# A gather that waits in mid-quad: two graph-attention layers with indirect DMA on Trainium2

## The chip, the core and the metric

The kernel runs on one NeuronCore of a Trainium2 chip. A core has five engines with a queue of instructions each: TensorE (PE in the profile, its weight loads PEld), VectorE (DVE), ScalarE (ACT), GpSimd (POOL) and SyncE (SP). They run side by side and wait for each other by semaphores only. Sixteen DMA engines move data between the chip's main memory (HBM) and the core's scratch memory (SBUF). The metric is the device time of one execution in microseconds (us), the median of several runs.

## The reference

A graph has 6250 nodes with 128 features and 106250 edges, sorted by target node. The first layer is an attention over the edges with 8 heads, followed by a feed-forward block; the second is another attention with 4 heads. Both have the same shape. Cut to what matters here, for the first:

```
q_dst = Q[dst] + rel_q[edge_type]
k_src = K[src] + rel_k[edge_type] + (time_emb @ Wt + bt)
v_src = V[src] + rel_v[edge_type]
euclid = sum(q_dst * k_src) / sqrt(DH) * decay
hyp    = -hyp_beta * norm(m[src] - m[dst]) * decay
logits = alpha * euclid + (1 - alpha) * hyp
attn   = softmax of logits over the edges with the same dst
agg    = segment_sum(v_src * attn, dst)
```

and for the second:

```
combined = leaky_relu(x_src[src] + x_dst[dst] + edge_emb[edge_type])
logits   = einsum(combined, att)
attn     = softmax of logits over the edges with the same dst
agg      = segment_sum(x_src[src] * attn, dst)
```

The rows that belong to `src` are scattered in memory, so they are gathered: one index, one row.

## The kernel before, in words

Edges are cut into tiles of 128, and four tiles (QS = 4) make a quad. A pass over all edges has 221 quads. There are two passes: `edges0` for the first layer and `edges1` for the second. Between them lie the joining of tiles and the work on nodes (`join_tiles`, `nodes0`), ahead of them the making of the tables (`front`), behind them `join_tiles` again and `nodes1`.

In a pass GpSimd does nothing but gather. For each quad it issues four indirect DMAs (line L1106 in the first pass, L1838 in the second), one for each tile. One gather fetches 128 rows from `d_table0` (384 floats each, 196.6 KB in all) or `d_table1` (132 floats each, 67.6 KB in all). All four add 16 to one semaphore, `rows_in[c % ring]`; it has its full value when all four have landed in SBUF. The rows go to a ring of 12 quads in the first pass (RQ0) and of 16 in the second (RQ). The names `gathered0` and `gathered` are these semaphores.

GpSimd waits for two things ahead of the first gather of a quad: that ScalarE has copied the indices (`idx_in`, once in four or eight quads) and that the quad which held the ring's slot is done (`sums`, which TensorE raises when it has summed that quad: two steps for a quad). Then comes a step on the semaphore `passed` that nobody waits for (`apart`), and the four gathers.

The other engines work on quad c in this order. TensorE's `edge(c)` waits for `rows_in` of the quad and adds gathered rows and rows of the target node, picked by a one-hot matmul, in PSUM (L1321 to L1333, L2014 and L2016). VectorE multiplies, reduces to logits and builds one-hots (L1161 to L1172, L1879 to L1898). Some quads later (LAG0 = 7 in the first pass, LAG = 10 in the second), with the weights of the softmax known, VectorE scales the values (L1196, L1895) and TensorE sums them by target (L1345, L2040). This raises `sums`. ScalarE copies the sums out of PSUM (L1275, L1981), and VectorE adds them to the accumulator (L1150, L1908). SyncE brings one-hot sources for two quads (first pass, L1058) or for eight quads (second pass, L1809 and L1811) as a broadcast of one row to 120 partitions.

Each pass is written as a head of two ring lengths, a hardware loop whose body is one ring length, and a tail, and so each engine has its own loop branch. The order of the instructions on each engine is the order in which the code emits them; no scheduler moves them.

Of the kernel before, what the change touches and what calls it, by code (L numbers as in the profile page):

```python
# [31 lines left out]
QS = 4  # L32
# [8 lines left out]
RQ = 16  # L41
# [3 lines left out]
LQ0, RQ0, LAG0, NQN = 4, 12, 7, 2  # L45
# [35 lines left out]
def apart(eng, passed):  # L81


    eng.sem_inc(passed, 1)
# [870 lines left out]
def nth0(i, c, per=1, plus=0):  # L955

    v = c * per + plus
    return v if i is None else i * (RQ0 * per) + v


def edges0(nc, k):
# [11 lines left out]
    with ExitStack() as ctx:  # L973
# [32 lines left out]
        rows_in = k.gathered0  # L1006
# [10 lines left out]
        def group(i, c, per=1, plus=0):  # L1017
            v = c // LQ0 * per + plus
            return v if i is None else i * (RQ0 // LQ0 * per) + v
# [5 lines left out]
        def quads(i, c0, emit):  # L1025
            for c in range(c0, c0 + (RQ0 if c0 else HEAD)):
                emit(i, c)
# [8 lines left out]
        with nc.Block() as block:  # L1036
# [60 lines left out]
            @block.gpsimd  # L1097
            def _(pl):
                def gather(i, c):
                    if c % LQ0 == 0:  # L1100
                        pl.wait_ge(idx_in, group(i, c, 1, 1))
                    if i is not None or c >= RQ0:
                        pl.wait_ge(sums, nth0(i, c - RQ0 + 1, 2))
                    apart(pl, k.passed)
                    for t in range(QS):
                        nc.gpsimd.indirect_dma_start(  # L1106
                            rows[:, c % RQ0 * QS + t, 0:3 * D], None, k.d_table0,
                            bass.IndirectOffsetOnAxis(ap=idx[c // LQ0 % 3][:, c % LQ0 * QS + t:c % LQ0 * QS + t + 1], axis=0))\
                            .then_inc(rows_in[c % RQ0], 16)

                quads(None, 0, gather)
                with pl.Fori(0, NITER) as i:
                    quads(i, HEAD, gather)
                for c in range(TAIL, sz.quads):
                    gather(None, c)
# [617 lines left out]
def nth(i, c, per=1, plus=0):  # L1733

    v = c * per + plus
    return v if i is None else i * (RQ * per) + v


def edges1(nc, k):
# [8 lines left out]
    with ExitStack() as ctx:  # L1748
# [27 lines left out]
        rows_in = k.gathered  # L1776
# [7 lines left out]
        def quads(i, c0, emit):  # L1784
            for c in range(c0, c0 + (RQ if c0 else HEAD)):
                emit(i, c)
# [11 lines left out]
        with nc.Block() as block:  # L1798
# [29 lines left out]
            @block.gpsimd  # L1828
            def _(pl):
                def gather(i, c):  # L1830
                    if c % LQ == 0:
                        pl.wait_ge(idx_in, c // LQ + 1 if i is None else i * 2 + (c // LQ + 1))
                    if i is not None or c >= RQ:
                        pl.wait_ge(sums, nth(i, c - RQ + 1, 2))
                    apart(pl, k.passed)
                    for t in range(QS):
                        r = c % RQ * QS + t
                        nc.gpsimd.indirect_dma_start(  # L1838
                            rows[:, r, :], None, k.d_table1,
                            bass.IndirectOffsetOnAxis(ap=idx[c // LQ % 2][:, c % LQ * QS + t:c % LQ * QS + t + 1], axis=0))\  # L1840
                            .then_inc(rows_in[c % RQ], 16)

                quads(None, 0, gather)
                with pl.Fori(0, NITER) as i:
                    quads(i, HEAD, gather)
                for c in range(NQUAD - RQ, sz.quads):
                    gather(None, c)
# [631 lines left out]
```

## Time and profile before

| | us |
|---|---|
| median of 3 timed runs | 3782.01 |
| lowest and highest of them | 3778.65, 3783.29 |
| span of the profiled execution | 3808.8 |
| first pass, first to last gather | 317.5 to 1830.5 |
| second pass, first to last gather | 2236.0 to 3602.8 |
| GpSimd busy in the whole span | 1924.7 (51%) |
| TensorE busy in the whole span | 2583.3 (68%) |
| VectorE busy in the whole span | 2475.7 (65%) |

The span runs from the first to the last instruction of one execution under the profiler; for that execution there is no other time. It is 26.8 us (0.7%) longer than the median of the timed runs. No engine is busy for three quarters of the span, so what matters is what the engines wait for. A line of a timeline has the start, the duration, the engine, the line of the code, the operation with what it writes and reads, and in brackets the idle time of that engine before it with what ended it. "remote" and "issue" there mean that the trace shows no releaser of its own; a releaser is inferred and can be another than the one named. The ends of matmuls are modelled.

### The profile page before, as it was taken

Reading aid. Unit: us, or ns where it says so; the run is one execution under the profiler, and the core shown is the slowest. Engines: PE = TensorE matmul, PEld = TensorE weight load, DVE = VectorE, ACT = ScalarE, POOL = GpSimd, SP = SyncE. Lnnn points to the kernel's source line nnn. Section 1 sums busy time; section 2 is a strip of 40 time slices with the busy share of each in tenths; the row PEclk is TensorE's granted clock in tenths of the full one; section 3 lists DMA queues with packets and bytes.
Section 4 is the critical chain, followed back from the end, with each engine's and each line's share of the span. In section 5 each row is a group of like instructions: output and inputs, shape, how many; then the busy total and the mean of one; then the engine's idle time right before and its main releaser. Section 6 shows DMA issues by size and latency. Waiting matters only on the chain. (4 is left out here: it accounts for less than half of the span.)

```text
span 3808.8 us, 60179 instructions
## 1 busy us (share of the span) xinstructions
PE 2583.3 (68%) x13302; PEld 1992.9 (52%) x13303; DVE 2475.7 (65%) x5935; ACT 1131.3 (30%) x3887; POOL 1924.7 (51%) x1957
## 2 busy tenths in 40 slices
PE   4893777777777777787668844666666566666654
PEld 3572555555555555565444423555555555555553
DVE  6443677677776767677755543666666666666678
ACT  2441444434343434444325520111111111111115
POOL 1004455555555555556330045666666666666554
PEclk9896888888888888898689977778788788878765
DMA  5475455555555555555301132333332333333221
GB/s 103 95 221 170 123 156 149 154 146 156 146 154 148 152 150 145 151 155 156 93 3 27 27 71 61 68 68 69 64 70 62 66 69 69 69 69 69 52 52 34
DMA packets 253667, 386.96 MB, mean 102 GB/s; under 512 B 70853, under 2 KB 168881, under 8 KB 249642
## 3 DMA queue, kind: packets, MB, share of 16 engines
q0 software_dynamic: 86432, 239.62, 24.7%
q1 hardware_dynamic: 132662, 130.96, 13.8%
q10 hardware_dynamic: 34260, 13.43, 1.4%
q14 instruction: 266, 2.18, 0.2%
q8 instruction: 47, 0.77, 0.1%
HBM read 342.88 MB, written 40.92 MB: 101 GB/s over the span
## 5 line engine op out<-in xcount | busy, mean ns | idle before, releaser
L1838 POOL DMA_INDIRECT pair<-d_table,e_idx x884 | 886.8, 1003 | 780.6 <-ACT e_idx L1962 300.6
L1106 POOL DMA_INDIRECT pair<-d_table,e_idx x884 | 870.5, 985 | 649.8 <-issue 238.6
L2040 PE MATMUL e_p_r<-pair,e_oh 128*122 128x132 f32 x1768 | 332.1, 342 | 425.5 <-DVE pair L1895 319.3
L1321 PE MATMUL e_p_t<-e_wbd,e_feat 128*128 128x512 f32 x442 | 289.1, 741 | 385.4 <-DVEq L1170 296.7
L2040 PEld LDWEIGHTS e_p_r<-pair,e_oh 128*122 128x122 f32 x1768 | 280.3, 233 | 467.3 <-issue 356.9
L1981 ACT COPY pair<-e_p_r 122x264 f32<-122x264 f32 x442 | 160.0, 380 | 994.2 <-DMA pair<-in_xT 471.9
L2014 PE MATMUL e_p_x<-pair,iden 128*128 128x264 f32 x884 | 342.8, 477 | 104.0 <-issue 63.2
L2016 PEld LDWEIGHTS e_p_x<-big,e_oht 128*128 128x128 f32 x1768 | 331.6, 232 | 48.9
L1325 PEld LDWEIGHTS e_p_q<-big,e_oht 128*128 128x128 f32 x1768 | 281.1, 226 | 136.5 <-issue 136.5
L1879 DVE SCALAR_TENSOR_TENSOR e_prod<-e_p_x,e_att 128x512 f32<-128x512 f32 x221 | 151.0, 683 | 271.6 <-remote 232.6
L2016 PE MATMUL e_p_x<-big,e_oht 128*128 x1768 | 325.6, 315 | 0.0
L1275 ACT COPY e_bound<-e_p_r 122x272 f32<-122x272 f32 x442 | 154.9, 387 | 512.6 <-remote 343.7
L1333 PEld LDWEIGHTS e_p_m<-big,e_oht 128*128 128x128 f32 x1768 | 240.2, 196 | 127.3 <-issue 127.3
L1283 ACT ACTIVATE e_p_m<-e_p_m 128x128 f32<-128x128 f32 x884 | 234.2, 265 | 205.1 <-ACT e_bound L1275 95.2
L1321 PEld LDWEIGHTS e_p_t<-e_wbd,e_feat 128*128 128x128 f32 x442 | 77.5, 219 | 406.3 <-issue 322.7
L1150 DVE TENSOR_TENSOR big<-big,e_bound 120x136 f32 x884 | 259.4, 293 | 36.5 <-issue 17.2
L1325 PE MATMUL e_p_q<-big,e_oht 128*128 x1768 | 279.1, 310 | 0.0
L1166 DVE TENSOR_TENSOR pair<-pair,e_p_q 128x512 f32<-128x512 f32 x221 | 150.5, 681 | 191.3 <-remote 187.5
L1908 DVE TENSOR_TENSOR big<-big,pair 120x132 f32 x884 | 217.6, 294 | 85.4 <-ACT pair L1981 39.9
L1161 DVE TENSOR_TENSOR pair<-pair,e_p_t 128x512 f32<-128x512 f32 x221 | 151.9, 687 | 183.9 <-issue 122.6
L1345 PE MATMUL e_p_r<-pair,e_oh 128*122 128x136 f32 x1768 | 251.7, 286 | 19.4 <-DVE pair L1196 10.1
L1331 PE MATMUL e_p_m<-pair,iden 128*128 128x512 f32 x442 | 256.9, 667 | 0.0
(362 smaller groups left out, 4518.6 us busy)
## 6 DMA issues: line engine op xcount, KB each, us to landing
pair<-d_table,e_idx POOLq DMA_INDIRECT x1768
e_node<-d_node SPq DMA_DIRECT2D x28, 960.0 KB
e_node<-d_node SPq DMA_DIRECT2D x111, 240.0 KB
d_table<-tab_kmv SPq DMA_DIRECT2D x54, 360.0 KB
e_feat<-in_edge_attr ACTq DMA_DIRECT2D x442, 16.0 KB
e_feat<-in_edge_attr SPq DMA_DIRECT2D x442, 16.0 KB
e_gate<-d_gate SPq DMA_DIRECT2D x84, 64.5 KB
d_decay<-pair SPq DMA_DIRECT2D x7, 512.0 KB, 4.1
```

The lines of the kernel that those rows point to most:

```text
L1106: nc.gpsimd.indirect_dma_start(rows[:, c % RQ0 * QS + t, 0:3 * D], None, k.d_table0, bass.IndirectOffsetOnAxis(ap=idx[c // LQ0 % 3][:, c % ...
L1150: last = V.tensor_tensor(to, to, bound[a // BQ % 3][0:BN, a % BQ * QS + t, :].unsqueeze(1), ALU.add)
L1283: last = A.activation(p_m[c % 2][:, t, :], p_m[c % 2][:, t, :], ACT.Square, accum_out=d2[c // LQ0 % 3][:, c % LQ0 * QS + t:c % LQ0 * QS + ...
L1321: M(p_t[:, :, :].rearrange("p t d -> p (t d)"), feat[c % 6][:, :], wbd[:, :, :].rearrange("p t d -> p (t d)"), start=True, stop=True).then ...
L1325: last = M(p_q[:, t, :], oht[c % 3][:, t * P:(t + 1) * P], qm[:, bass.ds(of[t], 1), 0:D], start=True, stop=True)
L1331: M(m[:, :, :], k.iden[:, :], rows[:, r:r + QS, D:2 * D], start=True, stop=False)
L1333: last = M(m[:, t, :], oht[c % 3][:, t * P:(t + 1) * P], qm[:, bass.ds(of[t], 1), D:2 * D], start=False, stop=(t == QS - 1))
L1345: last = M(p_r[h][0:R_LAST + 1, t - 2 * h, 0:W], oh[w % 2][:, t, :], rows[:, w % RQ0 * QS + t, 2 * D:R0], start=True, stop=True)
L1838: nc.gpsimd.indirect_dma_start(rows[:, r, :], None, k.d_table1, bass.IndirectOffsetOnAxis(ap=idx[c // LQ % 2][:, c % LQ * QS + t:c % LQ * ...
L2014: M(x[:, 2 * h:2 * h + 2, 0:W], k.iden[:, :], rows[:, r + 2 * h:r + 2 * h + 2, :], start=True, stop=False)
L2016: last = M(x[:, t, 0:W], oht[c % 4][:, t * P:(t + 1) * P], xd[:, bass.ds(held["blocks"][(c - 1) % 4 * QS + t if c else t], 1), :], start=F ...
L2040: last = M(p_r[h][0:R_LAST + 1, t - 2 * h, 0:W], oh[w % 2][:, t, :], rows[:, w % RQ * QS + t, :], start=True, stop=True)
```

## The change

In both passes GpSimd gets one more wait ahead of the third of the four gathers of quad c: until `rows_in` of quad c-1 has its full value, so until the four gathers of the quad before have landed. A step on `passed` follows it. The very first quad of a pass has no such wait. `slot` works out the value for the first pass; in the second it is written out.

```
@@ first pass
                     apart(pl, k.passed)
                     for t in range(QS):
+                        if t == QS // 2 and (i is not None or c >= 1):
+                            pl.wait_ge(rows_in[(c - 1) % RQ0], slot(i, c - 1, RQ0, 16 * QS))
+                            apart(pl, k.passed)
                         nc.gpsimd.indirect_dma_start(
                             rows[:, c % RQ0 * QS + t, 0:3 * D], None, k.d_table0,
@@ second pass
                     for t in range(QS):
                         r = c % RQ * QS + t
+                        if t == QS // 2 and (i is not None or c >= 1):
+                            b = c - 1
+                            pl.wait_ge(rows_in[b % RQ], 16 * QS * (b // RQ + 1) if i is None else i * (16 * QS) + 16 * QS * (b // RQ + 1))
+                            apart(pl, k.passed)
                         nc.gpsimd.indirect_dma_start(
                             rows[:, r, :], None, k.d_table1,
```

On GpSimd's queue this reads as follows in the loop of the first pass, from the loop's top. `e0_idx_in` is `idx_in`, `e0_sums` is `sums`, and `gathered0` with a number is `rows_in` of that slot. Before:

```order
L1112 ISA
L1103 ISA [waits e0_idx_in]
L1106 DMA pair<-d_table,e_idx 128x384 [waits e0_sums]
L1106 DMA pair<-d_table,e_idx 128x384 x3
L1103 REGISTER_ALU
L1106 DMA pair<-d_table,e_idx 128x384 [waits e0_sums]
L1106 DMA pair<-d_table,e_idx 128x384 x3
```

Now:

```order
L1115 ISA
L1103 ISA [waits e0_idx_in]
L1109 DMA pair<-d_table,e_idx 128x384 [waits e0_sums]
L1109 DMA pair<-d_table,e_idx 128x384
L1107 ISA
L1109 DMA pair<-d_table,e_idx 128x384 [waits gathered011]
L1109 DMA pair<-d_table,e_idx 128x384
L1103 REGISTER_ALU
L1109 DMA pair<-d_table,e_idx 128x384 [waits e0_sums]
L1109 DMA pair<-d_table,e_idx 128x384
L1107 REGISTER_ALU
L1109 DMA pair<-d_table,e_idx 128x384 [waits gathered00]
```

A quad's four gathers in a row are now two and two, with a wait and one register instruction between them. Nothing changes places, and no other engine's queue changes.

In the second pass the same stands in the loop. There the semaphores have numbers that earlier stages used under other names: `tab_x_in0` is `sums` and `tab_decay_out3` is `idx_in` of this pass. Before:

```order
L1838 DMA pair<-d_table,e_idx 128x132 [waits tab_x_in0]
L1838 DMA pair<-d_table,e_idx 128x132 x3
L1838 DMA pair<-d_table,e_idx 128x132 [waits tab_decay_out3,tab_x_in0]
L1838 DMA pair<-d_table,e_idx 128x132 x3
L1838 DMA pair<-d_table,e_idx 128x132 [waits tab_x_in0]
```

Now:

```order
L1851 ISA
L1837 ISA [waits tab_decay_out3]
L1845 DMA pair<-d_table,e_idx 128x132 [waits tab_x_in0]
L1845 DMA pair<-d_table,e_idx 128x132
L1843 ISA
L1845 DMA pair<-d_table,e_idx 128x132 [waits gathered15]
L1845 DMA pair<-d_table,e_idx 128x132
L1837 REGISTER_ALU
L1845 DMA pair<-d_table,e_idx 128x132 [waits tab_x_in0]
```

Here too each quad's gathers fall in two pairs, the second of them behind the landing of the quad before.

## Rows read from the trace of the kernel before

**Rows 1.** The page's head and its busy times (section 1).

```profile
span 3808.8 us, 60179 instructions
PE 2583.3 (68%) x13302; PEld 1992.9 (52%) x13303; DVE 2475.7 (65%) x5935; ACT 1131.3 (30%) x3887; POOL 1924.7 (51%) x1957
```

**Rows 2.** Windows over the two passes: length, busy time by engine, clock, DMA share, GB/s.

```profile
core 0: us, PE busy (x) PEld busy (x) DVE busy (x) ACT busy (x) POOL busy (x), PEclk, DMA share, GB/s
317.50:1830.50 1513.00, 1130.40 (x6160) 849.41 (x6161) 1059.73 (x2517) 600.09 (x2528) 870.47 (x884) 0.86 0.54 150
2236.00:3603.00 1367.00, 819.25 (x4317) 720.59 (x4317) 864.43 (x2180) 170.07 (x515) 886.76 (x884) 0.79 0.32 68
```

**Rows 3.** GpSimd's waits: line, released by, us in total, times, longest.

```profile
POOL pair L1838 <- issue: 244.1, 776, 2.0
POOL pair L1106 <- issue: 238.6, 727, 3.1
```

**Rows 4.** Waits of VectorE and ScalarE for TensorE's results, whole span.

```profile
DVE e_prod L1879 <- remote: 232.6, 38, 30.7
DVE pair L1166 <- remote: 187.5, 47, 7.0
ACT pair L1981 <- DMA pair<-in_xT: 471.9, 77, 11.8
ACT e_bound L1275 <- remote: 343.7, 103, 7.3
```

**Rows 5.** Timeline of the second pass, around one stall.

```profile
2850.67 0.33 SPq L1809 DMA_DIRECT2D e_node<-d_node  x1
...
2852.85 1.31 POOL L1838 DMA_INDIRECT pair<-d_table,e_idx  x1 [0.30 <-issue]
...
2855.72 0.94 POOL L1838 DMA_INDIRECT pair<-d_table,e_idx  x1 [0.30 <-issue]
...
2856.97 0.94 POOL L1838 DMA_INDIRECT pair<-d_table,e_idx  x1 [0.30 <-issue]
...
2859.43 0.61 PE L2016 MATMUL e_p_x<-big,e_oht 128*128 x4
...
2863.21 0.95 POOL L1838 DMA_INDIRECT pair<-d_table,e_idx  x1 [0.30 <-issue]
2866.20 0.69 DVE L1879 SCALAR_TENSOR_TENSOR e_prod<-e_p_x,e_att 128x512 f32<-128x512 f32 x1 [7.22 <-remote]
2866.38 0.66 ACT L1981 COPY pair<-e_p_r 122x264 f32<-122x264 f32 x2 [11.18 <-DMA pair<-in_xT]
...
2867.07 1.21 POOL L1838 DMA_INDIRECT pair<-d_table,e_idx  x1 [2.91 <-DMA pair<-in_xT]
```

**Rows 6.** Windows over the same place, columns as in rows 2.

```profile
2853.00:2854.00 1.00, 1.00 (x9) 1.00 (x10) 0.81 (x4) 0.28 (x1) 1.00 (x1) 1.00 1.01 217
2856.00:2857.00 1.00, 0.00 (x0) 0.00 (x0) 1.00 (x4) 0.00 (x0) 0.69 (x2) 1.00 1.12 214
2858.00:2859.00 1.00, 1.00 (x10) 0.94 (x9) 0.79 (x2) 0.00 (x0) 0.79 (x1) 1.00 0.68 152
2859.00:2860.00 1.00, 1.00 (x8) 0.79 (x6) 0.00 (x0) 0.00 (x0) 0.69 (x2) 1.00 0.19 50
```

**Rows 7.** Timeline of the first pass: a result taken up while GpSimd stands still.

```profile
1016.24 0.95 POOL L1106 DMA_INDIRECT pair<-d_table,e_idx  x1 [0.30 <-issue]
...
1017.00 1.09 PE L1345 MATMUL e_p_r<-pair,e_oh 128*122 128x136 f32 x8
...
1018.88 1.12 POOL L1106 DMA_INDIRECT pair<-d_table,e_idx  x1 [1.70 <-PE e_p_r L1345]
```

**Rows 8.** Timeline of the first pass: a result made while GpSimd gathers.

```profile
1030.74 1.09 PE L1345 MATMUL e_p_r<-pair,e_oh 128*122 128x136 f32 x8
...
1035.10 0.95 POOL L1106 DMA_INDIRECT pair<-d_table,e_idx  x1 [0.30 <-issue]
1037.66 0.69 DVE L1166 TENSOR_TENSOR pair<-pair,e_p_q 128x512 f32<-128x512 f32 x1 [5.50 <-remote]
1037.89 0.67 ACT L1275 COPY e_bound<-e_p_r 122x272 f32<-122x272 f32 x2 [5.30 <-remote]
```

**Rows 9.** Timeline of the second pass's start: gathers and the matmuls that wait for them.

```profile
2251.63 0.94 POOL L1838 DMA_INDIRECT pair<-d_table,e_idx  x1 [0.30 <-issue]
...
2254.36 0.88 PE L2014 MATMUL e_p_x<-pair,iden 128*128 128x264 f32 x2
```

**Rows 10.** The source line of the broadcast for eight quads.

```profile
L1809 SPq DMA_DIRECT2D e_node<-d_node x28: 330/337/539, 2232.6 to 3533.3; - x28
```

More of the change, by code:

```diff
@@ L1105, in gather @@
                     for t in range(QS):
+                        if t == QS // 2 and (i is not None or c >= 1):
+                            pl.wait_ge(rows_in[(c - 1) % RQ0], slot(i, c - 1, RQ0, 16 * QS))
+                            apart(pl, k.passed)
                         nc.gpsimd.indirect_dma_start(
@@ L1837, in gather @@
                         r = c % RQ * QS + t
+                        if t == QS // 2 and (i is not None or c >= 1):
+                            b = c - 1
+                            pl.wait_ge(rows_in[b % RQ], 16 * QS * (b // RQ + 1) if i is None else i * (16 * QS) + 16 * QS * (b // RQ + 1))
+                            apart(pl, k.passed)
                         nc.gpsimd.indirect_dma_start(
```

## The prediction

> **What bounds the kernel now.** I read the page's head first. No engine is busy for more than 68% of the span [rows 1], so waits decide. Next I asked for windows over the two passes, since only they change: 1513 us and 1367 us, together 2880 of 3808.8 us. With 221 quads each that is 6.85 and 6.19 us per quad. GpSimd is busy for 870 and 887 us of it, so it could finish a quad in 5.0 us (four gathers of 0.95 and four pauses of 0.30), and the DMA engines are busy to 0.54 and 0.32 [rows 2]. In neither pass is GpSimd or the DMA the limit on average.
>
> The view of waits by engine says who is late: VectorE waits 232.6 us at L1879 and 187.5 us at L1166, ScalarE 471.9 us at L1981 and 343.7 us at L1275 [rows 4]. All four lines read PSUM, that is, they wait for TensorE. But TensorE is not at work then either. The timeline shows it best. In the second pass the last matmul of a quad starts at 2859.43; VectorE, which waits for it, starts at 2866.20 and ScalarE at 2866.38. Between them only GpSimd works; its last gather of that series ends at 2864.16, and it too goes on only at 2867.07 [rows 5]. In the first pass the sums are made at 1030.74 to 1031.83, GpSimd gathers until 1036.05, and VectorE and ScalarE go on at 1037.66 and 1037.89 [rows 8]. The opposite case: GpSimd's gather ends at 1017.19, the sums end at 1018.09, and GpSimd itself takes them up 0.79 us later [rows 7]. So a result of TensorE that comes late in an unbroken series of gathers is taken up some 1.6 to 2.0 us after the series has ended, and one that comes while GpSimd rests is taken up at once. Why this is so no row says. I call such a stretch a stall; it is the costliest thing in both passes, and its length goes with GpSimd's series. That is where a wait on GpSimd can act.
>
> **The change part by part.** It adds 220 waits and 220 steps on `passed` to each pass, removes nothing and moves no instruction. Other engines' queues are as before.
>
> The instructions themselves: the pause between two gathers is 0.30 us, and it is also 0.30 us ahead of a quad that needs no wait, where a wait and a step stand already [rows 5]. I cost 440 of them at nothing; GpSimd's own 0.95 us of work on the gather before hides them. Without that cover it would be at most the 0.79 us from a release to the gather's start [rows 7].
>
> Behind the new wait stand the third and fourth gather and the next quad. Who needs them? Quad c is released in the first pass when quad c-12 is summed, in TensorE's step c-4, and read in step c-1, three steps or some 20 us later; in the second pass it is c-6 to c-1, some 31 us. Its gathers take 5 us. A delay of 1 to 4 us is hidden from `rows_in`'s readers.
>
> How long does the wait last? The third gather starts 2.80 us after the end of the last gather of the quad before (0.30 + 1.25 + 1.25) if GpSimd did not rest, and later if it did. The last gather of quad 1 of the second pass ends at 2252.57 and TensorE reads it at 2254.36 [rows 9], so it lands within 1.79 us. With 0.79 us for the release that is 2.58 us: under 2.80, no delay. Of 884 gathers in this pass 776 start after a mere pause, so 108 are behind a wait and 113 quads start without one [rows 3]; all quads are covered while the DMA engines are free. In the first pass the rows are three times as long. No row shows a landing there. From below it is 1.79 us as well; from above I add 129 KB at the 217 GB/s of a full window [rows 6], 0.6 us, and have 2.39 + 0.79 = 3.18 us, a delay of 0.4 us. With the middle, 0.2 us, for the 884 - 727 = 157 waits and so 64 quads without a rest [rows 3], GpSimd loses 13 us of its 640 us of idle time. Where such a quad stands in a stall, the stall lasts that much longer. I take 3 us on the path (from 0 to 26).
>
> The Trainium skill, in DMA: Bandwidth & Descriptors, "Anatomy of one DMA", gives a gather a fixed 2.0 us and its bytes at 436 GB/s, so 2.45 us in the first pass and 2.16 us in the second. By this rule every back-to-back quad would be held, by 0.44 and 0.15 us, in sum some 45 us on GpSimd. The trace has at most 1.79 us in the second pass and disagrees there; for the first pass no row decides.
>
> The exception is the broadcast for eight quads in the second pass. It is issued at 2850.67 [rows 5]; the DMA engines are full at 2853 and 2856 and still at 0.68 at 2858, and only at 2859 down to 0.19 [rows 6]. The last gather of the quad before ends at 2854.16 in the midst of it. I take it to land near 2858, where the load falls off. Then the third gather of the next quad starts at 2858.9 instead of 2856.97: 1.9 us late, behind 2.2 us of rest on GpSimd (0 to 4 us by the same window). A rest of 1.6 to 2.0 us is what lets TensorE's results through. So the series of gathers that ran to 2864.16 is cut in two. Here the result of 2859.4 to 2860 comes two gathers after the rest instead of five or more into a series, and VectorE need not stand for 7.22 us. The second half still has six gathers and ends about 2 us later, so part of a stall can come back. I take 4 us saved of the 7.22 for each such place (bounds: 7.2 saved, 1.9 lost).
>
> How many places? There are 28 broadcasts [rows 10]; one is ahead of the loop. GpSimd is at work in 0.65 of the pass [rows 2], so some 17 of 27 meet a series, and I count 15. That is 15 x 4 = 60 us saved. I expect a third back: time saved makes the series follow each other more closely, and 5.0 us of gathers per quad against 6.19 us leaves little rest. So -60 + 20 + 3 = -37 us.
>
> The profiled span is 26.8 us longer than the median of the timed runs; the sum is a difference, and I apply it to either: 3808.8 to about 3772 in a profile, 3782 to 3745 us timed.
>
> **The rivals.** *Nothing happens.* The waits are met before they are reached, and the rests behind the broadcasts fall where GpSimd would have rested anyway or are too short. For it: 2.58 against 2.80 us, and 20 us of slack. Against it: the full DMA windows. Time: 3782 us.
>
> *Longer stalls, slower.* If a rest of some 2 us inside a series does not let results through (say, because what counts is that GpSimd has nothing left to do), the series just ends later, and every stall with it. The place is the gather series behind a broadcast and the back-to-back quads of the first pass. The price is 27 x 1.9 = 51 us and up to 64 x 0.4 = 26 us. It decides as soon as a delayed series still holds VectorE to its end plus 2 us. With half of both on the path it is +38: 3820 us. For it: both stalls in the rows ended after the series, and I have no row with a rest of 2 us in the middle of one. Against it: [rows 7], where a rest of under 1 us was enough.
>
> *Much faster.* If it is the number of gathers handed over ahead that matters, not GpSimd's rest, then the wait caps it at four in every quad, and stalls shrink everywhere. VectorE's waits of 232.6 and 187.5 us [rows 4] halved give -210: about 3570 us. For it: in the stalls shown GpSimd had the gathers of a further quad in hand, and no row excludes it. Against it: GpSimd's own starts would hardly move, and all that I can see goes by them.
>
> **How the numbers follow.** I give the forecast 0.46, nothing 0.21, slower 0.23, much faster 0.10. About 0.2%, 7.6 us, is what a measurement of this kernel can tell from no change. Faster by more than that is the forecast and the last case, less a little where the gain given back is all of it: 0.54. Within it: 0.23. Slower: 0.23. The forecast's own range is 3700 (all 27 places, 3 us each) to 3774. The range takes in "nothing" and most of "slower": 3690 to 3812 us, with some 0.1 left out on either side.
>
> **What would show it right or wrong.** In the changed kernel's profile the third gather behind a broadcast should have an idle time of about 2 us ahead of it, and there should be 15 to 25 such in the second pass and few over 1 us in the first. VectorE's wait at L1879 (some lines lower now) should fall from 232.6 by about 40 us and ScalarE's at L1981 likewise, and the second pass from 1367 to about 1327 us; the first should stay within 5 us of 1513. If instead the waits at L1879 and L1981 grow with the rests there, the slower rival holds. If the first pass falls by more than 20 us, my account of what ends a stall is wrong, since almost no rest is added there. If no idle time appears ahead of third gathers, the change does not reach the gathers at all.

## The result and the profile after

The changed kernel takes 3818.49 us (median of 4 runs, 3812.17 to 3826.65); the kernel before took 3782.65 us beside it (4 runs, 3778.65 to 3785.65). The ratio is 1.0098, 95% interval 1.0074 to 1.0122: slower by 36 us. A repetition with more runs gave 1.0092 (1.0072 to 1.0112). The forecast was 3745 us, and 3818 lies just above its range.

The page's head, to be held against [rows 1]:

```profile
span 3810.3 us, 60671 instructions
PE 2566.5 (67%) x13302; PEld 1979.6 (52%) x13303; DVE 2470.3 (65%) x5935; ACT 1130.8 (30%) x3887; POOL 1919.9 (50%) x1957
```

The two profiled spans, 3808.8 and 3810.3 us, hide the difference. Before's profiled execution was 27 us longer than its timed median, after's 8 us shorter. So I compare stages, and look how much each scatters among kernels that have it unchanged. The windows over the passes of the changed kernel, columns as in [rows 2]:

```profile
core 0: us, PE busy (x) PEld busy (x) DVE busy (x) ACT busy (x) POOL busy (x), PEclk, DMA share, GB/s
304.70:1796.60 1491.90, 1123.29 (x6158) 841.08 (x6159) 1056.29 (x2519) 600.02 (x2534) 870.27 (x884) 0.89 0.54 152
2198.90:3607.60 1408.70, 822.33 (x4332) 723.27 (x4333) 865.85 (x2185) 171.86 (x517) 881.81 (x884) 0.78 0.30 66
```

The first pass shrank from 1513 to 1492 us. That says nothing: in the 14 other kernels run below with an unchanged first pass it took 1483 to 1533 us. The second pass grew from 1367 to 1409 us; in a run below with the second pass unchanged it took 1356 us, and in two more with the wait 1401 and 1404 us. That is the loss.

GpSimd's waits, to be held against [rows 3] (line, released by, us in total, times, longest):

```profile
POOL pair L1109 <- issue: 264.4, 731, 2.2
POOL pair L1845 <- issue: 240.9, 760, 3.8
...
POOL pair L1845 <- DMA pair<-in_xT: 135.7, 51, 4.4
POOL pair L1845 <- DMA pair<-d_table,e_idx: 90.2, 42, 5.9
...
POOL pair L1109 <- DMA pair<-d_table,e_idx: 20.3, 14, 3.0
```

A releaser is new: the landing of gathers (`pair<-d_table`), 90.2 us in the second pass. By the trace 24 third gathers of that pass have over 1.5 us of idle time ahead of them (median 3.8, longest 5.9 us), 23 of them at quads with c % 8 = 2, behind the broadcast. In the first pass 10 have over 1.5 us.

What waited for TensorE in [rows 4], now:

```profile
DVE e_prod L1886 <- remote: 149.1, 23, 32.3
DVE pair L1169 <- remote: 129.6, 33, 7.1
ACT pair L1988 <- DMA pair<-in_xT: 440.4, 76, 15.4
ACT e_bound L1278 <- remote: 328.0, 106, 6.0
```

All four fell, and yet the kernel is slower. Only one of these falls is clear of the scatter. L1166 (now L1169) and L1275 (now L1278) belong to the first pass, and in the 14 kernels run below with an unchanged first pass the same rows read 123 to 178 us and 244 to 346 us. A row holds one releaser only: over all releasers L1981 waits 992 us before, 978 us in the run below with an unchanged second pass and 981 us now. L1879 over all releasers waits 271 us before and 278 and 280 us in two kernels below without a wait in the second pass, and 220 us now (202 us in the repetition): this fall is real. The time went to other lines. VectorE's waits from 2330 to 3560 us, first of the kernel before:

```profile
DVE e_prod L1879 <- remote: 165.4, 32, 13.5
...
DVE e_fwd L1919 <- DMA pair<-in_xT: 44.7, 8, 11.0
DVE big L1908 <- ACT pair L1981: 37.1, 30, 3.8
DVE big L1908 <- issue: 32.0, 50, 1.8
```

and of the changed kernel:

```profile
DVE e_prod L1886 <- remote: 91.3, 19, 11.4
DVE e_fwd L1926 <- DMA pair<-in_xT: 86.7, 12, 10.7
DVE big L1915 <- ACT pair L1988: 61.3, 30, 6.7
DVE big L1915 <- issue: 55.9, 63, 4.4
```

The wait ahead of the product (L1886) gave 74 us; those of the scan (L1926) and of the additions (L1915) took 42, 24 and 24 us. The scan waits for TensorE's transpose, the additions for ScalarE's copy of TensorE's sums; the releasers named are inferred. So results of TensorE are still late, only others than before. Over the whole second pass VectorE's idle time is 494 us in the kernel before and 480 us in the run below with an unchanged second pass, and 529 to 536 us in the three traces with the wait in every quad.

Where in the period of eight quads this happens: VectorE's step (from one start of L1879, now L1886, to the next; mean over quads 24 to 215, us), by c % 8:

| c % 8 | 0 | 1 | 2 | 3 | 4 | 5 | 6 | 7 | sum |
|---|---|---|---|---|---|---|---|---|---|
| before | 8.37 | 5.40 | 4.72 | 5.28 | 6.76 | 5.18 | 6.87 | 6.60 | 49.2 |
| changed | 9.76 | 7.98 | 5.75 | 6.40 | 6.40 | 4.70 | 4.20 | 5.66 | 50.9 |
| changed, repeated | 10.01 | 8.53 | 4.67 | 6.33 | 6.01 | 5.04 | 4.27 | 5.67 | 50.5 |

On average VectorE reads a quad 19 to 26 us after its last gather has ended, so it works some four quads behind GpSimd, and GpSimd's rest at c % 8 = 2 falls in VectorE's steps 6 and 7. These became 3.6 us shorter, which fits results that come through in the rest. Steps 0 to 3 became 6.1 us longer. One such place in the timeline of the changed kernel:

```profile
3027.36 0.33 SPq L1812 DMA_DIRECT2D e_node<-d_node  x1
...
3029.54 1.31 POOL L1845 DMA_INDIRECT pair<-d_table,e_idx  x1 [0.30 <-issue]
...
3037.49 1.33 POOL L1845 DMA_INDIRECT pair<-d_table,e_idx  x1 [4.12 <-DMA pair<-d_table,e_idx]
...
3050.89 0.27 PE L2040 MATMUL e_p_e<-iden,e_ext 128*128 128x128 f32 x1
...
3059.22 0.94 POOL L1845 DMA_INDIRECT pair<-d_table,e_idx  x1 [0.30 <-issue]
3060.22 0.30 DVE L1915 TENSOR_TENSOR big<-big,pair 120x132 f32 x1 [2.50 <-issue]
...
3063.13 0.27 ACT L1979 COPY pair<-e_p_e 128x128 f32<-128x128 f32 x1 [12.66 <-DMA pair<-in_xT]
...
3064.00 1.18 POOL L1845 DMA_INDIRECT pair<-d_table,e_idx  x1 [3.83 <-DMA pair<-in_xT]
```

The broadcast is issued at 3027.36, the last gather of quad 129 is issued at 3029.54, and GpSimd rests 4.12 us. Then it gathers without a rest from 3037.49 to 3060.16, 18 gathers. ScalarE has stood still for 12.66 us when it goes on at 3063.13; by the trace the result of TensorE that it waits for (L2040) was ready at 3051.16, 12.0 us earlier. GpSimd rests 3.83 us, and the next round begins. The windows of one us over this broadcast:

```profile
3030.00:3031.00 1.00, 1.00 (x10) 0.97 (x9) 0.70 (x4) 0.38 (x1) 0.85 (x1) 1.00 1.03 213
3034.00:3035.00 1.00, 1.00 (x9) 0.98 (x9) 0.70 (x3) 0.28 (x2) 0.00 (x0) 1.00 0.99 89
3035.00:3036.00 1.00, 1.00 (x8) 0.92 (x7) 0.85 (x2) 0.38 (x2) 0.00 (x0) 1.00 0.38 93
3036.00:3037.00 1.00, 0.74 (x6) 0.52 (x4) 1.00 (x3) 0.00 (x0) 0.00 (x0) 1.00 0.00 0
```

The DMA engines (share, the last number but one) are full in the window from 3034, at 0.38 in the one from 3035 and idle in the one from 3036. With 0.79 us from release to start, GpSimd's wait was met at 3036.7. So the gathers land about when the last of the broadcast does.

A series is a run of gathers with no idle time of over 0.5 us between them. In the trace of the kernel before no series that begins in quads 24 to 220 is longer than 12 gathers; in the changed one 10 have 16 or more (nine of 18, one of 22), and all ten begin with the third gather behind a broadcast. I count these, as long series, in each run below.

### The profile page after: what moved, and what is told of

Read it like the earlier page. It is cut to its first block and busy times, and to the rows that moved or that the text cites. A ratio compares the mean times of both kernels' runs of the same rounds, so it can differ in the third digit from the quotient of the medians.

```text
span 3810.3 us, 60671 instructions
## 1 busy us (share of the span) xinstructions
PE 2566.5 (67%) x13302; PEld 1979.6 (52%) x13303; DVE 2470.3 (65%) x5935; ACT 1130.8 (30%) x3887; POOL 1919.9 (50%) x1957
## 5 line engine op out<-in xcount | busy, mean ns | idle before, releaser
L1915 DVE TENSOR_TENSOR big<-big,pair 120x132 f32 x884 | 217.9, 294 | 132.9 <-ACT pair L1988 65.3
L1886 DVE SCALAR_TENSOR_TENSOR e_prod<-e_p_x,e_att 128x512 f32<-128x512 f32 x221 | 151.0, 683 | 220.5 <-remote 149.1
L1278 ACT COPY e_bound<-e_p_r 122x272 f32<-122x272 f32 x442 | 154.9, 387 | 464.9 <-remote 328.0
L1334 PE MATMUL e_p_m<-pair,iden 128*128 128x512 f32 x442 | 249.0, 648 | 0.0
L1336 PE MATMUL e_p_m<-big,e_oht 128*128 x1768 | 237.9, 276 | 8.9 <-issue 8.8
```

The costliest lines, as they stand in the source:

```text
L1334: M(m[:, :, :], k.iden[:, :], rows[:, r:r + QS, D:2 * D], start=True, stop=False)
L1336: last = M(m[:, t, :], oht[c % 3][:, t * P:(t + 1) * P], qm[:, bass.ds(of[t], 1), D:2 * D], start=False, stop=(t == QS - 1))
```

## The experiments

Each change is made to the kernel before unless said otherwise, in the second pass unless said otherwise. Ratios are to the kernel before on the same chip. That kernel took 3776 to 3788 us beside most of them and 3825 us beside one group (the first runs with small transfers, and the rests at c % 8 = 6 and in every second quad), so only ratios are compared. `rest(...)` is short for a wait on `rows_in[c % RQ]` and a step on `passed`.

**Which waits cost.** The wait in the first pass alone:

```diff
@@ edges0 only
+ if t == QS // 2 and (i is not None or c >= 1): wait for rows_in of c-1
```

> The wait in the first pass alone. Theory A (the loss is made in the second pass, where 24 third gathers rest 1.5 to 5.9 us behind the broadcast for eight quads): 3780 us, within 8 us of before. Rival B (the loss is spread over every added wait and step, 440 of them, 36 us): 3800 us. Rival C (the loss is made in the first pass, and the profiled 1513 us of before was an outlier): 3818 us.

Measured: 0.9996 (0.9977 to 1.0015). The wait in the first pass costs nothing.

The wait in the second pass alone:

```diff
@@ edges1 only
+ if t == QS // 2 and (i is not None or c >= 1): wait for rows_in of c-1
```

> The wait in the second pass alone. Theory A (the loss is made there): 3818 us, the whole of the changed kernel's loss. Rival B (every added instruction costs alike): 3800 us. Rival C (the first pass): 3782 us.

Measured: 1.0104 (1.0075 to 1.0132), 11 series of 16 or more. All of the loss is here.

```diff
- if t == QS // 2 and (i is not None or c >= 1):
+ if t == QS // 2 and (i is not None or c >= 1) and c % LQ == 2:
```

> Second pass alone, and of its 220 waits only the 28 of quads c with c % 8 = 2, those behind the broadcast for eight quads. Theory A: 3818 us with 28 waits instead of 440, and rests of 1.5 to 6 us ahead of those third gathers. Rival B: under 3 us more than before. The mechanism of my forecast (a rest inside a series shortens the stall) would show as a time under 3782 us.

Measured: 1.0106 (1.0080 to 1.0132), 8 long series. GpSimd's waits of this run have the landings 22 times:

```profile
POOL pair L1842 <- DMA pair<-d_table,e_idx: 60.7, 22, 5.7
```

```diff
- if t == QS // 2 and (i is not None or c >= 1):
+ if t == QS // 2 and (i is not None or c >= 1) and c % LQ != 2:
```

> Second pass alone, 192 waits: all but those behind the broadcast. Theory A: 3782 us, within 8 us, and no rests ahead of third gathers over 1 us except at one or two quads. Rival A2 (the rest only moves on to the next quad's third gather, c % 8 = 3): rests and a loss of 10 to 30 us. Rival B: 3798 us.

Measured: 1.0020 (0.9997 to 1.0043), 1 long series; 7 third gathers rest over 1 us. So 28 of the 440 waits make the loss, and neither the number of instructions (rival B) nor the waits elsewhere do.

**Is it the large transfer?** The changed kernel with the broadcast in four parts:

```diff
- sp.dma_start(node[u][0:BN, :], <row of 8 quads>.broadcast_to(...)).then_inc(node_in[u], 16)
+ def piece(p):   # a quarter of the columns; for p > 0 ahead of it:
+     sp.wait_ge(oht_built, nth(i, c - LQ + 2 * p))
+     sp.dma_start(node[u][0:BN, a:b], <row>[a:b].broadcast_to(...)).then_inc(node_in[u], 16)
- dve.wait_ge(node_in[u], 32 * ...)
+ dve.wait_ge(node_in[u], 80 * ...)
```

> The changed kernel (the wait in both passes), but SyncE brings the one-hot source for eight quads of the second pass in four transfers of 0.24 MB, two quads of VectorE's work apart, instead of one of 0.96 MB. Theory A (the waits cost time only because the one large transfer holds back the landing of the gathers issued with it): the 23 rests of 1.5 to 6 us become rests of at most 1.5 us and the loss goes: equal to the kernel before with the same four transfers, within 8 us. Rival D (any rest behind a transfer costs, and four transfers make four rests): 3820 us or more.

Measured: 1.0003 (0.9988 to 1.0019), no long series; one third gather rests over 1.5 us. The same kernel on another chip:

> The changed kernel with four small transfers once more, on the chip of the other runs of this call. If the transfer of 0.96 MB is what makes the waits dear: within 0.3% of before. If the earlier result was a matter of its chip: 1.008 or more.

Measured: 0.9997 (0.9979 to 1.0015). With the same waits and a smaller transfer the loss is gone. GpSimd waits for landings as often as in the changed kernel, but briefly:

```profile
POOL pair L1854 <- DMA pair<-d_table,e_idx: 18.4, 49, 2.1
```

The kernel before with the same four parts, as the base:

> The kernel before with the same four transfers, as the base for the run beside it. No added wait. If nobody waits for the landings in time: 3776 us, within 8 us. If the late landings behind the large transfer already cost the kernel before something on TensorE: 5 to 20 us less.

Measured: 1.0005 (0.9987 to 1.0022). The late landings cost nothing where nobody waits for them. And the changed kernel beside other runs:

> The changed kernel once more, since the runs of the four transfers came from a chip on which the kernel before takes 3825 us and not 3776: beside the others of this call. Theory A: 1.010 times before. If the loss were a matter of the chip: within 0.2% on some.

Measured: 1.0092 (1.0072 to 1.0112), 8 long series.

**Does a rest cost by its place, its length, or with the broadcast?** A rest away from the broadcast:

```diff
+ if t == QS // 2 and c % LQ == 6: rest(2 of this quad's gathers landed)
```

> The kernel before with a rest of GpSimd in the second pass away from the broadcast: ahead of the third gather of quads c with c % 8 = 6 it waits until the first two gathers of the same quad have landed (1.3 us median landing and 0.79 us for the release, so about 2 us of rest at 28 places, 50 us of GpSimd's time). Theory A (a rest delays the series, and what stands behind the series is late by as much): 15 to 50 us slower, 3791 to 3826 us. The mechanism of my forecast (a rest of 2 us lets TensorE's results through): faster, 3720 to 3760 us. Theory A1 (a rest costs only when it is much longer than 2 us, since then several quads of slots come free and the next series is 18 gathers long): 3776 us, within 8 us.

Measured: 1.0026 (1.0006 to 1.0046), 1 long series; rests of 2.4 us (median) at 27 places. These 10 us lie between theory A (15 to 50) and theory A1 (at most 8); the time did not fall. The same rest where the changed kernel has it, with small transfers:

```diff
@@ with the broadcast in four parts
+ if t == QS // 2 and c % LQ == 2: rest(2 of this quad's gathers landed)
```

> Small transfers, and a rest of 2.3 us at c % 8 = 2 (until two gathers of the same quad have landed), so where the changed kernel rests, but made without the large transfer. Theory P (the place in the period of eight quads decides; a rest there pushes the series under the chain of scans and exponentials of c % 8 = 0 and 1): 1.008 to 1.012, as with the 28 waits behind the broadcast, whose rests are in sum as long. Theory B (rest of GpSimd and the broadcast must come together): 1.000 to 1.004, as at c % 8 = 6.

Measured: 1.0033 (1.0014 to 1.0052), 2 long series. The cost is about the same at both places. But VectorE's step 0 is 10.8 us here and steps 6 and 7 are 4.2 and 5.8 us: the same pattern as in the changed kernel, with a smaller sum. The long rest at the first place:

```diff
+ if t >= 2 and c % LQ == 6: rest(t of this quad's gathers landed)
```

> The kernel before with a rest of about 4.3 us in the second pass at quads with c % 8 = 6: ahead of the third gather until two and ahead of the fourth until three of the same quad have landed (28 places, two rests of about 2.3 and 2.0 us instead of one of 2.3, which cost 1.0026). Theory A1 (the cost grows faster than the rest, since more slots come free during a long one and the next series is longer): 1.008 to 1.012, as behind the broadcast. Theory P (what counts is the place in the period of eight quads, and c % 8 = 6 is a cheap one): 1.003 to 1.005.

Measured: 1.0109 (1.0082 to 1.0136), 8 long series; two rests of 2.3 us, 4.1 us beyond the usual pauses. And at the other place without the large transfer:

```diff
@@ with the broadcast in four parts
+ if t >= 2 and c % LQ == 2: rest(t of this quad's gathers landed)
```

> Small transfers, and at c % 8 = 2 of the second pass the long double rest (ahead of the third gather until two and ahead of the fourth until three of the same quad have landed, 28 x 4.1 us beyond the usual pause). Theory N (length alone decides, neither the place nor the broadcast): 1.008 to 1.012, as at c % 8 = 6 with the large transfer. Theory B (it takes the large transfer too): 1.002 to 1.005.

Measured: 1.0114 (1.0093 to 1.0135), 15 long series. So neither the broadcast nor its place is needed for a loss of this size: 27 or 28 rests of 2.1 us beyond the pause cost 10 and 12 us, as many of 4.1 us (in two halves, with one gather between) cost 41 and 43 us. For twice the rest that is about four times the cost, roughly, since the intervals of the short rests reach from 2 to 20 us. The length is not the whole account. With the 28 waits behind the broadcast alone the third gathers there rest 54 us beyond the pause in all, in the one execution that was traced, at 20 places and up to 5.7 us each, and this costs 40 us; the 28 short rests at the same quads are 60 us in all and cost 12. Whether the longest single rests or the large transfer itself make this difference no run separates.

**Rest or delay?** Work in place of the long rest:

```diff
+ if t >= 2 and c % LQ == 6:
+     nc.gpsimd.memset(spin[:, :], 0.0).then_inc(spun, 1)   # 128x2048
```

> The kernel before, and in the second pass at c % 8 = 6 GpSimd fills a scratch tile of 128x2048 ahead of the third and once more ahead of the fourth gather, some 2 us each, where the long rest stood: 28 x 4 us of work instead of rest. If a rest gives something back because TensorE's results come through in it, work costs more than the rest's 1.0109: 1.014 to 1.030. If only the delay of GpSimd's gathers counts: 1.009 to 1.013, and the results of TensorE that come during the fill are taken up late like those in a series of gathers or not at all differently; if the fill lets them through, it is the handing over of gathers that holds them.

Measured: 1.0082 (1.0063 to 1.0102), 4 long series: just under the range for the delay alone, with a delay of 3.4 instead of 4.1 us. The fill's row (line, operation, count, busy, mean ns, idle before):

```profile
L1844 POOL MEMSET pair<- 128x2048 f32 x54 | 98.3, 1821 | 0.0
```

A fill puts the next gather 1.98 instead of 0.30 us after the one before, so each place delays by 3.4 us, 91 us in all, and costs 31 us; the long rest there delayed by 110 us and cost 41. That is 0.34 and 0.37 us for each us, but it does not show that work and rest cost alike, for the fill does more than delay gathers. VectorE's one-hot (L1866 in the kernel before, L1873 here) takes 0.49 us (median) and never over 0.73 us where no fill runs. The 23 that overlap a fill take up to 2.77 us, 22.5 us more in all than their number times 0.49. How much of the 31 us comes from this is open. The timeline of one fill bears on what holds TensorE's results:

```profile
2374.72 2.33 DVE L1873 TENSOR_SCALAR e_oht<-e_node,part 128x512 f32<-128x512 bf16 x1
...
2374.94 1.82 POOL L1844 MEMSET pair<- 128x2048 f32 x1
2375.01 1.06 PE L2047 MATMUL e_p_r<-pair,e_oh 128*122 128x132 f32 x8
2375.66 0.83 ACT L1988 COPY pair<-e_p_r 122x264 f32<-122x264 f32 x2 [2.87 <-PE e_p_r L2047]
```

ScalarE takes up TensorE's sums in the midst of GpSimd's work, long before it ends at 2376.76. Nine results for which ScalarE waited over 0.5 us came during a fill, and all nine were taken up 0.04 us after their end. VectorE is another matter: one result that it waited for, in the pass's opening series, was taken up 5.4 us after its end, and three that came during a fill were taken up 0.52 us late because VectorE was itself in one of the long one-hots. So no fill held a result back from ScalarE, and my premise for this run, that work blocks and rest doesn't, fell for it; for VectorE's one-hot it did not.

How much do nine of nine show? Without fills, promptness depends on how far the series of gathers has run when the result comes. I count the results of TensorE that ScalarE waited for in the second pass, from quad 24 on. In the kernel before, 92 of 119 that come during a series' first four gathers are taken up within 0.1 us, during the fifth and sixth 33 of 64, from the seventh on none of 45 (median 5.1 us late). In the changed kernel these are 85 of 112, 21 of 54 and 7 of 50 (median 3.6 us late). Of the nine results in a fill, three came after two gathers and two after three gathers and the first fill, where a series would have let most through as well. The other four came after six gathers, where at most half are prompt without a fill. So the evidence that the fill lets results through rests on these four.

**Can the long series be cut, and does that gain?**

```diff
+ if t == QS // 2 and (i is not None or c >= 1) and c % LQ == 2: wait for rows_in of c-1
+ if t == QS // 2 and c % LQ == 4: rest(2 of this quad's gathers landed)
```

> The 28 waits behind the broadcast alone (1.0106 by themselves, with series of up to 18 gathers after each rest) and one more rest of about 2.3 us at the third gather of quads with c % 8 = 4, until two gathers of that quad have landed; it cuts the long series in two. Theory L (the loss comes from the long series that follows the rest): less than before that cut, 1.000 to 1.007, although GpSimd loses 60 us more. Theory A (each rest puts everything later): 1.013 to 1.025.

Measured: 1.0118 (1.0096 to 1.0140). The second rest cut the series behind the first, but there are still 7 long ones, and all begin with the gather behind the second rest. VectorE's long steps went from 0 and 1 to 2 and 3 (8.6 and 7.8 us). The 45 us are less than theory A's 50 to 95 and more than theory L allows. Theory L is neither shown nor refuted by it, since the series stayed long.

```diff
+ if t == QS // 2 and c % 2 == 0: rest(2 of this quad's gathers landed)
```

> The same rest in every second quad of the second pass: no series is longer than 8 gathers. GpSimd alone would need 2 x 5.0 + 1.7 = 11.7 us for two quads, 1295 us for the pass, so it isn't the bound. Theory A (rests are added to the path): 50 to 190 us slower. The rival (it is the length of an unbroken series that makes stalls, and series of 8 are too short for long ones): 3600 to 3740 us.

Measured: 1.0046 (1.0029 to 1.0063), no series over 8. Neither expected range held. Here 111 rests of 2.3 us (median) cost 18 us, less for each than the 28. But GpSimd never waits for a free slot any more: the whole idle time ahead of first gathers is 67 us, 0.30 for each. It has become the bound, so what the shorter series gave can't be read off.

```diff
@@ with the broadcast in four parts
+ if t == 1 and (i is not None or c >= 1): wait for rows_in of c-1
```

> With the four small transfers, and in the second pass the wait for the quad before ahead of the second gather of every quad instead of the third: a rest of about 0.8 us in each of 221 quads, none of over 2.5 us. GpSimd needs 5.6 of the 6.2 us per quad, so it isn't the bound. If many short rests let TensorE's results through and the series stay at 4 gathers: 0.96 to 0.99 times before. If a rest of 0.8 us is too short for that: 1.00 to 1.02. The rest in every second quad took 300 us from what ScalarE and VectorE wait, but made GpSimd the bound.

Measured: 1.0022 (1.0001 to 1.0042), series of 4. My arithmetic for GpSimd was off: the rests are 1.32 us in the mean (median 1.07), not 0.8, and it is the bound again, with 0.30 us ahead of each first gather.

```diff
@@ with the broadcast in four parts
+ if t == 1 and (i is not None or c >= 1) and c % 2 == 0: wait for rows_in of c-1
```

> Small transfers, and in every second quad of the second pass the wait for the quad before ahead of the second gather (1.3 us of rest in the run that had it in all quads and in which GpSimd became the bound at 6.23 us per quad). GpSimd needs 5.0 and 6.2 us, 5.6 on average, and no series is over 8 gathers. Theory L (length of a series is the cost): 0.97 to 0.99 times before. If series of 8 already hold TensorE's results back as much: 1.00 to 1.01.

Measured: 1.0022 (1.0002 to 1.0041). No series is over 9, GpSimd has 112 us of idle time to spare ahead of first gathers (179 less 67), and nothing is gained. Series shorter than those of the kernel before are no remedy.

```diff
+ if i is not None or c >= 8:
+     pl.wait_ge(x_read, nth(i, c - 3))   # ahead of the quad's first gather
```

> The kernel before, with one more wait ahead of the first gather of a quad of the second pass: until VectorE has read the sums of quad c-4, so GpSimd is held at most about four quads ahead of VectorE. Slots that come free in a rest can't be used up in one series then. If the length of a series is what a stall costs: series of at most 8 to 10 gathers and 0.95 to 0.99 times before. If GpSimd's lead is needed: 1.00 to 1.05.

Measured: 1.0257 (1.0233 to 1.0280), the slowest of all. Tied closer to VectorE, GpSimd stands when VectorE stands (rests of 4.5 and 4.8 us at c % 8 = 1 and 4) and makes up for it in 23 series of 16 gathers. I had expected series of 8 to 10; the ratio itself is in the range for "GpSimd's lead is needed".

No kernel tried beats the one before.

**All runs side by side** (ratio, and series of 16 or more gathers among quads 24 to 220 in its profile):

| second pass | ratio | long series |
|---|---|---|
| unchanged, or only small transfers | 0.9996, 1.0005 | 2, 1 |
| waits with small transfers | 1.0003, 0.9997 | 0, 1 |
| waits but those behind the broadcast | 1.0020 | 1 |
| rest of 2 us, 27 and 28 times | 1.0026, 1.0033 | 1, 2 |
| series held to 4, 9 and 8 | 1.0022, 1.0022, 1.0046 | 0, 0, 0 |
| work, delay of 3.4 us, 27 times | 1.0082 | 4 |
| waits behind the broadcast, alone and with others | 1.0098, 1.0092, 1.0104, 1.0106, 1.0118 | 10, 8, 11, 8, 7 |
| rest of 4 us, 27 and 28 times | 1.0109, 1.0114 | 8, 15 |
| tied to VectorE | 1.0257 | 23 |

Every kernel that is slower by 0.8% or more has at least 4 long series, every other one at most 2. The order within the groups is not strict. The lateness of ScalarE's results (from TensorE's end to ScalarE's start, summed over quads from 24 on) is 333 us in the kernel before, 364 us in the run with the first pass's wait alone and 334 us with only small transfers, and 365 to 384 us in the three traces with the wait in every quad; in the changed kernel 130 of its 381 us fall in the ten long series. The scatter among unchanged kernels nearly reaches the changed ones, so this points one way but is no proof. That the long series are the cause, and not a second sign of the delay, is argued from the timeline and these counts, not shown: no run had long rests without long series.

## Why the prediction was wrong

**The instructions cost nothing: right.** 192 waits and steps in one pass cost 1.0020 with an interval that holds 1; 220 in the first pass 0.9996.

**The readers of the rows don't notice: right.** In the changed kernel VectorE still reads a quad 19 us or more after its gathers on average at each place of the period, and never, in quads 24 to 215, less than 10.9 us.

**How long the waits last: right away from the broadcast, too short behind it.** I had 2.58 us from a quad's last gather to a third gather that is released by its landing. Where a run waits for that landing ahead of the second gather in each quad, this gather starts 2.34 us (median) after the last one's end: covered, as forecast. The Trainium skill (DMA: Bandwidth & Descriptors, "Anatomy of one DMA") gives a fixed 2.0 us and the bytes at 436 GB/s. The estimate from it is 2.16 us, and 2.95 us with the 0.79 us for the release if it is counted from the end of GpSimd's instruction; counted so, the trace disagrees. In the first pass I forecast 13 us of waiting; the idle time ahead of third gathers is 110 us against 67, 43 us, and it cost nothing all the same. Behind the broadcast I took 2.2 us (0 to 4) at 15 of 27 places and measured a median of 3.8 us at 23. Two of the 28 broadcasts are issued ahead of the first gather, so 26 fall in the pass, and nearly all of them meet a series. The windows gave the right moment (the end of the broadcast's load), but I read it from a single one.

**The step that failed: "I take 4 us saved of the 7.22 for each such place", with a third given back.** Its first half happened: the two steps of VectorE that the rest falls in became 3.6 us shorter, and the wait at L1879 fell by 83 us (by 51 over all releasers) where I had said 40. But I booked this as saved time and put the price of GpSimd's delay at a third of it. The runs show that it is all given back and more: VectorE's steps 0 to 3 became 6.1 us longer. Even a rest of about the length that I had assumed, 2.3 us, costs 0.3% instead of saving 1%, at the place of the change and elsewhere. The long rests, behind the broadcast or elsewhere, moved VectorE's long steps to other quads, and the sum of its eight steps grew from 49.2 us (49.0 in the run with an unchanged second pass) to between 50.1 and 50.9 us.

**Why the delay is paid for although nobody waits for the rows.** GpSimd has idle time to spare ahead of first gathers, 275 us less 67 in the second pass, and should take a delay back out of it. It does only in part. With the rests of 2.1 us at c % 8 = 2 the idle time ahead of third gathers is 60 us longer than in the kernel before and that ahead of first gathers 46 us shorter (229 against 275). In the changed kernel these are 79 and 30 us. GpSimd's busy time hardly changes, so what is not taken back is the growth of the pass over again and not its reason. The reason I give is this. During a rest of 4 us VectorE and TensorE go on and free further slots; so GpSimd then mostly gathers 16 to 18 times without a rest, where 12 was the most in the trace of the kernel before and 16, once or twice, in two others without a wait in the second pass. Results that come from the seventh gather of a series on lie for 3.6 us (median) in the changed kernel, as counted above. That this sum is what the 36 us consist of is the argued step.

**The rival that came true** is "longer stalls, slower": 3820 us by half of 27 x 1.9 and half of 64 x 0.4. Its place behind the broadcast is right, and half on the path is what was measured there (36 of 79 us); the first pass's part was nothing. Its reason, that a rest doesn't let results through, fits only in part: VectorE's steps under the rest did become shorter, but the series behind the rest still holds VectorE and ScalarE until some 2.9 us after its end (3060.16 to 3063.1 above), which was this rival's own sign. I gave it 0.23 against 0.46, because [rows 7] showed a prompt result during a rest. They showed that a rest helps the results in it; they could not show what the next series does to the others.

**What I said would show it:** 15 to 25 rests in the second pass came, but longer, and 18 over 1 us in the first, where I had said few; L1879 fell, L1981 hardly (472 to 440 us, 992 to 981 over all releasers); the second pass did not fall to 1327 but rose to 1409. The first pass fell by 21 us, more than the 20 that I had set as a sign against my account of the stalls. With unchanged first passes between 1483 and 1533 us this sign can decide nothing, and I should have set it against that scatter. "Much faster" is out: with small transfers the wait caps the gathers ahead in every quad just so, and the ratio is 1.

## What to carry to other kernels

A wait of one line that falls is no gain until the sum of all waits of that engine in the same stretch has fallen; look which line took it over. Before you add a wait for a landing, find the largest transfer that can stand ahead of it: 28 of 440 waits made the whole loss, and four smaller transfers undid it. The producer here, which has slack, took short rests for little and long ones dearly (60 us in 28 short rests cost 12 us, 115 us in as many long ones 43 us), so cost a delay by its length at each place and not by its sum alone. And work put in place of a wait is no neutral delay: look whether it slows another engine.

## What the runs showed of the hardware

How late ScalarE takes up a result of TensorE goes by the place in the series of gathers under way: 0.04 us (median) during the first four gathers, 5.1 us from the seventh on in the kernel before. In every trace here with series of seven or more gathers the two medians are 0.04 us and 1.4 us or more. While GpSimd fills memory for 1.8 us, nine of nine are taken up after 0.04 us, four of them after six gathers. So GpSimd's being busy alone does not hold them. Why a series does, no run here tells.

VectorE's one-hot of 128x512 from bf16 takes 0.49 us, also during gathers, and up to 2.77 us when GpSimd fills memory at the same time.

Late in a long series VectorE's register instructions slow down too: in the trace such instructions, 0.04 to 0.08 us otherwise, took 0.70 us each, most of them from about the ninth gather on. In quads 24 to 215 of the second pass there are 24 of these in the kernel before, 43 in the changed one and 82 in the one with long rests at c % 8 = 2, but only 4 in the one with long rests at c % 8 = 6, which is as slow. So they don't explain the loss. They make up part of the gaps between additions that the timeline above calls "issue": two of them, 1.4 us, stand in the 2.50 us ahead of 3060.22.
